# The end of a four-sublayer transformer kernel: last shared tile, late sums, row numbers and store queues rearranged

## The chip, the cores and the metric

The kernel runs on one core of one Trainium2 chip, in one launch. The metric is the device time of the whole program in microseconds (us). The engines of the core are TensorE (PE in the profile), VectorE (DVE), ScalarE (ACT), GpSimd (POOL) and SyncE (SP); each runs its own instruction stream, and they meet only at semaphores.

## What is computed

Two layers on 896 tokens of width 512, each a cross attention and a feed-forward part with residual sums. Only the last part, the mixture of experts of layer 1, matters here:

```
scores = softmax(t @ gate_w.T); weights, indices = top_k(scores, 2)
y = 0
for e in range(16):
    w_e = sum(where(indices == e, weights, 0))
    y = y + swiglu(t, w1[e], w3[e], w2[e]) * w_e
z = swiglu(t, sw1, sw3, sw2)
x = x + tanh(g_ffn[1]) * (y + z)
```

Every token goes to two of 16 experts (y) and through the shared pair of experts (z). All arithmetic is float32.

## The kernel before, in words

The 896 tokens are NT = 7 tiles of P = 128 rows; x, the residual and later the output, stays on chip as [128, 7, 512]. Before the experts run, each token row is scattered by expert into an array in DRAM (sorted_rows), so that the experts work on dense tiles of 128 rows, at least one for each expert; in this input there are 21.

One expert tile n goes through these hands. GpSimd loads its rows (`load`), ScalarE copies them (`place`), TensorE turns them (`rows_T`), multiplies (`up_expert`), turns the hidden rows (`hidden_T`) and multiplies again (`down_expert`). VectorE copies the result from PSUM to the one buffer yr (`tile_out`, semaphore d_sv). GpSimd then copies the tile's row numbers to to_row and issues an indirect DMA that scatters yr to y_dram, called token_rows in the profile (`scatter`, semaphore y_st). There is one yr and one to_row, so `tile_out(n)` waits until scatter n-1 has landed. The row numbers themselves were written by VectorE earlier (`row_ends`, semaphore row_read).

The shared experts' second product is `shared_part(t, ...)` on TensorE for token tile t: 18 matmuls of 512 columns (6 chunks of the inner width, three products each), which leave a sum in PSUM bank SHARED_BANK[t]. VectorE adds it to x in `shared_out(t)` (semaphore y_sv). Tiles 0 to 3 (BEFORE = 4) are multiplied around the start of the expert tiles, tiles 4 to 6 at TensorE's very end, after and between the last expert products. SHARED_BANK is (4, 5, 0, 1, 0, 1, 2), so tile 6 is alone in bank 2; still, `shared_part` waits at every t from 2 on for the shared_out two tiles back, for tile 6 that of tile 4.

Each token has two scattered results, j = 0 and j = 1. SyncE loads them back tile by tile: seven loads of 256 KB for j = 0 when all tiles but the last expert's have landed, seven for j = 1 when everything has (`back[t][j]`, semaphores back_ld). VectorE adds the seven of j = 0, then goes through the tiles for j = 1: for t below 4 only the add (semaphore out_st), for t = 4, 5 and 6 first `shared_out(t)` and then the add. SyncE stores each tile to out when out_st reaches it, and then waits for all seven stores.

The order on every engine is written out by hand in the code.

Of the kernel before, what the change touches and what calls it, by code (L numbers as in the profile page):

```python
# [28 lines left out]
P = 128  # L29
# [4 lines left out]
TOK = B * S  # L34
NT = TOK // P
# [17 lines left out]
BEFORE = 4  # L53
# [7 lines left out]
def flamingo(nc, x_in, ctx_in, mask_in, cols_in, rows_in, scal_in, wq0_in, wk0_in, wv0_in, wo0_in,  # L61
             gu0_in, wd0_in, wq1_in, wg1_in, wkv1_in, wo1_in, gate_in, sh13_in, sh2_in,
             e13_in, e2_in, out):
    with ExitStack() as stack:
# [3 lines left out]
        def sem(name):  # L68
            return stack.enter_context(nc.semaphore(name))
# [43 lines left out]
        x = nc.alloc_sbuf_tensor_at("x", [P, NT, D], F32, offset=x_base)  # L113
# [10 lines left out]
        def at(off, *dims, rows_=P):  # L124
            n = 1
            for d in dims:
                n *= d
            return shaped(arena[0:rows_, off:off + n], dims)
# [118 lines left out]
        back = [[at(28144 + t * D, D), at(4352 + t * D if t < 5 else 44288 + (t - 5) * D, D)] for t in range(NT)]  # L247
# [29 lines left out]
        y_dram = nc.dram_tensor("token_rows", (P + 2 * TOK, D), F32, kind="Internal").ap()  # L277
# [21 lines left out]
        x_ld = sem("x_ld")  # L299
# [89 lines left out]
        d_sv = sem("d_sv")  # L389
        y_st = sem("y_st")  # L390
# [3 lines left out]
        row_read = sem("row_read")  # L394
        to_set = sem("to_set")
        to_held = sem("to_held")
        back_add = sem("back_add")
        out_st = sem("out_st")
# [7 lines left out]
        back_ld = [[sem(f"back_ld{t}_{j}") for j in range(2)] for t in range(NT)]  # L406
# [3 lines left out]
        def counts(engine):  # L410

            return [engine.value_load(tile_count[0:1, i:i + 1], min_val=NE - 3 + i, max_val=ROWS_MAX - 3 + i)
                    for i in range(4)]
# [31 lines left out]
            return lnt0[:, n % 6, :] if n < NT else lnt1[:, n % NT % 4, :] if n < 2 * NT else lnt[:, n % 2, :]  # L445


        @block.sync
        def _(sp):

# [88 lines left out]
            tiles = sp.value_load(tile_count[0:1, 3:4], min_val=NE, max_val=ROWS_MAX)  # L539
            for j, landed in enumerate((last, tiles)):  # L540
                sp.wait_ge(y_st, landed * 16)
                for t in range(NT):
                    first = P + j * TOK + t * P
                    sp.dma_start(back[t][j], y_dram[first:first + P, :]).then_inc(back_ld[t][j], 16)
            out_t = out.rearrange("(t p) d -> t p d", p=P)
            for t in range(NT):
                sp.wait_ge(out_st, 1 + t)
                sp.dma_start(out_t[t], x[:, t, :]).then_inc(x_ld, 16)
            sp.wait_ge(x_ld, 16 * (NT + 1))
# [3 lines left out]
        def _(pe):  # L553
# [133 lines left out]
            for i in range(8):  # L687
                n, m = i // 4, i % 4
# [258 lines left out]
            pe.wait_ge(w_low, nth("sh2"))  # L947

            def shared_part(t, first, end):
                if first == 0 and t >= 2:  # L950
                    pe.wait_ge(y_sv, 3 * NT + t - 1)
                into = ps[:, SHARED_BANK[t], :]
                for m in range(first, end):
                    z = SH_CHUNKS[m]
                    if t == 0:
                        pe.wait_ge(hsh_low, m + 1)
                    h, w = ([half[0:z, t * P:(t + 1) * P] for half in hsh[m][:2]],
                            [half[0:z, m, :] for half in sh2[:2]])
                    if t >= BEFORE:
                        w[0] = sh2_kept[0:z, m, :]  # L960
                        if m == 4:
                            h[1] = h4_kept[0:z, (t - BEFORE) * P:(t - BEFORE + 1) * P]
                    mm(into, h[0], w[0], start=m == 0, stop=False)  # L963
                    mm(into, h[0], w[1], start=False, stop=False)
                    last = mm(into, h[1], w[0], start=False, stop=m == 5)
                if end == 6:
                    last.then_inc(y_mm, 1)

            for t in range(BEFORE - 1):
                shared_part(t, 0, 6)  # L970

            pe.wait_ge(tables_set, 1)
            last3, last2, last1, tiles = counts(pe)
# [36 lines left out]

            rows_T(0)
            shared_part(BEFORE - 1, 0, 3)
            up_expert(0)
            rows_T(1)
            shared_part(BEFORE - 1, 3, 6)
            hidden_T(0)
            with pe.Fori(1, last1) as n:
# [16 lines left out]
        def _(act):  # L1034
# [95 lines left out]
            for i in range(8):  # L1130
                n, m = i // 4, i % 4
# [128 lines left out]
            for i in range(8):  # L1260
                n, m = i // 4, i % 4
# [47 lines left out]
            last3, last2, last1, tiles = counts(act)  # L1309

            def rows_save(n):
                act.wait_ge(xg_tr, n + 1)
                fn(xgT, ps[:, 6, :].rearrange("p (k t) -> p k t", k=KC), ACT.Copy).then_inc(xg_sv, 1)

            def silu_tile(n):
                act.wait_ge(gu_mm, n + 1)
                fn(smoe, ps[:, 4, 0:EI], ACT.Silu).then_inc(m_silu, 1)
# [16 lines left out]
            silu_tile(last2)  # L1334
            rows_save(last1)
            silu_tile(last1)


        @block.vector
        def _(dve):  # L1340
# [448 lines left out]
            def shared_out(t):  # L1789
                dve.wait_ge(y_mm, 3 * NT + t + 1)  # L1790
                if t >= BEFORE:
                    dve.wait_ge(back_add, t + 1)
                v.scalar_tensor_tensor(x[:, t, :], ps[:, SHARED_BANK[t], :], tg[:, 3:4], x[:, t, :], ALU.mult, ALU.add
                                       ).then_inc(y_sv, 1)
# [5 lines left out]
            last3, last2, last1, tiles = counts(dve)  # L1800
# [49 lines left out]
            for t in range(NT):  # L1850
                dve.wait_ge(back_ld[t][0], 16)
                v.tensor_tensor(x[:, t, :], x[:, t, :], back[t][0], ALU.add).then_inc(back_add, 1)
            for t in range(NT):
                if t >= BEFORE:
                    shared_out(t)
                dve.wait_ge(back_ld[t][1], 16)
                if t < BEFORE:
                    dve.wait_ge(back_add, t + 1)
                else:
                    dve.wait_ge(y_sv, 3 * NT + t + 1)  # L1860
                v.tensor_tensor(x[:, t, :], x[:, t, :], back[t][1], ALU.add).then_inc(out_st, 1)
# [3 lines left out]
        def _(pool):  # L1865
# [24 lines left out]
            for i in range(8):  # L1890
                n, m = i // 4, i % 4
# [31 lines left out]
            last3, last2, last1, tiles = counts(pool)  # L1923
# [11 lines left out]
                load(n)  # L1935

            def scatter(n, stored=None):
                pool.wait_ge(d_sv, n + 1)
                if stored is not None:
                    pool.wait_ge(y_st, stored)  # L1940
                nc.gpsimd.tensor_copy(to_row[:], arena[:, bass.ds(A_TO + n % 4, 1)]).then_inc(to_set, 1)
                pool.wait_ge(to_set, n + 1)
                pool.sem_inc(to_held, 1)
                pool.indirect_dma_start(y_dram, bass.IndirectOffsetOnAxis(to_row[:, 0:1], 0), yr, None
                                        ).then_inc(y_st, 16)
# [4 lines left out]
            next_load(2)  # L1950
            next_load(3)
            scatter(0)
            next_load(4)
            scatter(1, 16)
            with pool.Fori(5, tiles) as n:
                next_load(n)
                scatter(n - 3, n * 16 - 48)
# [61 lines left out]
```

## Time and profile before

| | us |
|---|---|
| median of 3 runs | 962.27 |
| lowest and highest | 962.15, 965.42 |
| the profiled execution, its own time | 964.5 |
| its span, first to last instruction | 962.8 |
| TensorE busy in the span | 932.7 |

The profiled execution's own time lies 1.7 us above its span. The profile is of one execution, so durations from it are compared with that execution's time first and then set against the median.

### The profile page before, as it was taken

The numbers are of one execution on the slowest core, as the hardware profiler recorded it, in microseconds if no ns is written. First come the engines' busy times: TensorE is split into PE (matmuls) and PEld (weight loads), VectorE is DVE, ScalarE is ACT, GpSimd is POOL, SyncE is SP. The second block draws the span as 40 slices with busy tenths as digits, with TensorE's granted clock in tenths as the row PEclk, the third lists the DMA queues.
The fourth block names the chain that finished last, engine by engine and source line by source line (L and its number), as shares of the span: only waits on it lengthen the run. The fifth ranks groups of instructions, "written<-read, shape, count | busy, mean of one in ns | idle before, by whom it ended". The sixth has DMA issues, their size and how long they took to land.

```text
span 962.8 us, 17950 instructions
## 1 busy us (share of the span) xinstructions
PE 932.7 (97%) x7523; PEld 720.6 (75%) x7524; DVE 451.6 (47%) x755; ACT 303.0 (31%) x477; POOL 76.9 (8%) x110
## 2 busy tenths in 40 slices
PE   5999999999999999989999999999999999999995
PEld 5878787878788888779999544888798766666554
DVE  6665545455455456873221154597665122222224
ACT  4633333332332334653211121335532222222210
POOL 0000000000000003000000000112006112122210
PEclk9999999999999999999999999999999999999998
DMA  8000010101011012044000300840503449787534
GB/s 338 10 27 34 1 34 1 34 1 34 5 74 34 1 35 78 2 154 175 1 1 1 131 1 0 318 182 1 181 1 131 156 170 329 285 290 241 210 123 166
DMA packets 26773, 96.04 MB, mean 100 GB/s; under 512 B 3282, under 2 KB 4306, under 8 KB 23634
## 3 DMA queue, kind: packets, MB, share of 16 engines
q1 hardware_dynamic: 20354, 72.69, 21.3%
q0 software_dynamic: 6352, 22.35, 6.2%
q8 instruction: 55, 0.90, 0.4%
q14 instruction: 12, 0.10, 0.0%
HBM read 76.37 MB, written 18.66 MB: 99 GB/s over the span
## 4 chain that ended last, share of the span: by engine, by line
PE 88%; DVE 6%; ACT 3%; DMA 2%; issue 1%; SPq 0%; POOL 0%; POOLq 0%; DVEq 0%; ACTq 0%
PE ps L563 18%; PE ps L564 17%; PE ps L565 17%; PE ps L991 10%; PE ps L827 7%; PE ps L1001 5%; PE ps L643 4%; PE ps L626 4%; PE ps L849 1%; PE ps L982 1%; DMA land_c<-in_ctx 1%; PE ps L665 1%; PE ps L963 1%; PE ps L612 1%; PE ps L1008 1%
## 5 line engine op out<-in xcount | busy, mean ns | idle before, releaser
L563 PE MATMUL ps<-arena_r 128*125 128x512 f32 (+1 forms) x416 | 163.8, 394 | 4.2 <-DVE arena_r L1357 4.2
L564 PE MATMUL ps<-arena_r 128*125 128x512 f32 (+1 forms) x416 | 157.0, 377 | 0.0
L565 PE MATMUL ps<-arena_r 128*125 128x512 f32 (+1 forms) x416 | 156.8, 377 | 0.0
L563 PE MATMUL ps<-hT,arena_r 128*128 128x448 f32 (+1 forms) x368 | 136.3, 370 | 2.4 <-DVE arena_r L1376 1.1
L565 PE MATMUL ps<-hT,arena_r 128*128 128x448 f32 (+1 forms) x368 | 134.4, 365 | 0.0
L564 PE MATMUL ps<-hT,arena_r 128*128 128x448 f32 (+1 forms) x368 | 134.4, 365 | 0.0
L991 PE MATMUL ps<-arena 128*128 x336 | 102.9, 459 | 0.0
L1062 ACT ACTIVATE arena<-arena,mbias,mscale 125x448 f32<-125x448 f32 x96 | 66.2, 752 | 102.0 <-DVE arena L1484 101.9
L563 PEld LDWEIGHTS ps<-arena_r 128*125 128x125 f32 (+1 forms) x416 | 78.0, 188 | 21.8 <-DVE arena_r L1357 4.6
L565 PEld LDWEIGHTS ps<-arena_r 128*125 128x125 f32 (+1 forms) x416 | 77.9, 187 | 13.8
L564 PEld LDWEIGHTS ps<-arena_r 128*125 128x125 f32 (+1 forms) x416 | 78.1, 188 | 10.7
L991 PEld LDWEIGHTS ps<-arena 128*128 128x128 f32 x336 | 62.3, 190 | 31.2
L563 PEld LDWEIGHTS ps<-hT,arena_r 128*128 128x128 f32 (+1 forms) x368 | 68.3, 186 | 10.8 <-issue 1.9
L565 PEld LDWEIGHTS ps<-hT,arena_r 128*128 128x128 f32 (+1 forms) x368 | 68.3, 186 | 6.4
L564 PEld LDWEIGHTS ps<-hT,arena_r 128*128 128x128 f32 (+1 forms) x368 | 68.3, 186 | 6.1
L827 PE MATMUL ps<-arena 128*128 128x512 f32 x154 | 66.9, 592 | 0.0
L1484 DVE TENSOR_SCALAR arena<-ps 125x1344 f32<-125x1344 f32 x32 | 49.8, 1557 | 20.3 <-PE ps L626 20.0
L1001 PE MATMUL ps<-arena 128*128 (+1 forms) x126 | 57.7, 594 | 0.5 <-DVE arena L1819 0.5
L827 PEld LDWEIGHTS ps<-arena 128*128 128x128 f32 x154 | 28.9, 190 | 34.5 <-issue 34.4
L1616 DVE SCALAR_TENSOR_TENSOR arena<-ps,cols,arena 128x896 f32<-128x896 f32 x11 | 12.7, 1151 | 77.1 <-ACT arena L1218 77.1
L1808 DVE SCALAR_TENSOR_TENSOR arena<-ps,arena 128x352 f32<-128x352 f32 x21 | 12.3, 584 | 73.2 <-PE ps L991 47.0
L643 PEld LDWEIGHTS ps<-arena 125*32 125x32 f32 x1536 | 35.7, 110 | 12.0 <-issue 11.6
(224 smaller groups left out, 1167.0 us busy)
## 6 DMA issues: line engine op xcount, KB each, us to landing
arena<-in_e SPq DMA_DIRECT2D x16, 1408.0 KB, 6.6
arena<-in_e SPq DMA_DIRECT2D x16, 512.0 KB, 7.4
sorted_rows<-arena POOLq DMA_DIRECT2D x1, 7453.0 KB, 34.0
land_c<-in_ctx SPq DMA_DIRECT2D x8, 752.0 KB, 4.2
arena<-sorted_rows POOLq DMA_DIRECT2D x21, 257.0 KB, 6.1
land_w<-in_gu SPq DMA_DIRECT2D x8, 512.0 KB, 5.3
arena<-token_rows SPq DMA_DIRECT2D x14, 256.0 KB, 4.5
arena<-in_e SPq DMA_DIRECT2D x16, 192.0 KB, 8.8
```

Of the source, the lines that this page charges most:

```text
L563: mm(into, a[0], w[0], start=i == 0, stop=False)
L564: mm(into, a[0], w[1], start=False, stop=False)
L565: last = mm(into, a[1], w[0], start=False, stop=i == len(operands) - 1)
L626: last = mm(ps[0:TP, h, c * S:(c + 1) * S], kT[key_half][r, g, c * TP:(c + 1) * TP], queries[query_half][r, b, g, :], start=i == 0, stop=i ...
L643: last = mm(ps[h * HD:(h + 1) * HD, 7, first:first + S], w, probs[g % 2][:, h, c * S:(c + 1) * S], start=c == 0, stop=c == TC - 1)
L827: last = mm(into, h0[m][:, t * P:(t + 1) * P], wd0[:, m, :], start=m == 0, stop=m == MC - 1)
L991: last = mm(ps[:, 4 + j, 0:EI], xgT[:, k, :], arena[:, bass.ds(w + (k * 2 * EI + j * EI), EI)], start=k == 0, stop=k == KC - 1)
L1001: last = mm(ps[:, 3, :], hmoeT[0:z, c, :], arena[0:z, bass.ds(w + (2816 + c * D), D)], start=c == 0, stop=c == 2)
L1062: done = fn(p, p, ACT.Exp, bias=mbias[:, b * 3 + c:b * 3 + c + 1], scale=mscale[:, b * 3 + c:b * 3 + c + 1])
L1484: v.tensor_scalar(probs[g % 2], ps[0:TP, 0:HG, 0:TC * S], -CLIP / SCALE, CLIP / SCALE, ALU.max, ALU.min).then_inc(clipped, 1)
L1616: v.scalar_tensor_tensor(into[0:size].rearrange("p (n t) -> p n t", n=2), ps[0:size, 4 * (1 - m % 2) + 2:4 * (1 - m % 2) + 4, 0:HALF], sca ...
L1808: v.scalar_tensor_tensor(hmoe[:, 0:EI], ps[:, 5, 0:EI], weight, smoe, ALU.mult, ALU.mult).then_inc(m_h, 1)
```

## The change

Four edits, all in the program's last 30 us or so and in the code that the expert tiles share:

1. `shared_part(6)` no longer waits for `shared_out(4)`.
2. VectorE does `shared_out(4)` and `shared_out(5)` right after the seven adds of j = 0, ahead of all adds of j = 1. `shared_out(6)` stays where it was.
3. GpSimd's `scatter(n)` waits first for row_read (the row numbers are written) and for the scatter before, makes to_row, and only then waits for d_sv (the result is in yr). One more increment of to_held, for which nobody waits, stands between; the DMA follows the second one.
4. The loads of j = 1 and the stores of the odd tiles (1, 3, 5) are issued by ScalarE, those of the even tiles (0, 2, 4, 6) by SyncE.

```diff
--- before.py
+++ after.py
@@ -539,11 +542,10 @@
             for j, landed in enumerate((last, tiles)):
                 sp.wait_ge(y_st, landed * 16)
-                for t in range(NT):
+                for t in range(0, NT, 1 + j):
                     first = P + j * TOK + t * P
                     sp.dma_start(back[t][j], y_dram[first:first + P, :]).then_inc(back_ld[t][j], 16)
-            out_t = out.rearrange("(t p) d -> t p d", p=P)
-            for t in range(NT):
+            for t in range(0, NT, 2):
                 sp.wait_ge(out_st, 1 + t)
                 sp.dma_start(out_t[t], x[:, t, :]).then_inc(x_ld, 16)
             sp.wait_ge(x_ld, 16 * (NT + 1))
@@ -947,7 +949,7 @@
             def shared_part(t, first, end):
-                if first == 0 and t >= 2:
+                if first == 0 and 2 <= t < NT - 1:
                     pe.wait_ge(y_sv, 3 * NT + t - 1)
@@ -1335,6 +1337,14 @@
             rows_save(last1)
             silu_tile(last1)
 
+            act.wait_ge(y_st, tiles * 16)
+            for t in range(1, NT, 2):
+                first = P + TOK + t * P
+                act.dma_start(back[t][1], y_dram[first:first + P, :]).then_inc(back_ld[t][1], 16)
+            for t in range(1, NT, 2):
+                act.wait_ge(out_st, 1 + t)
+                act.dma_start(out_t[t], x[:, t, :]).then_inc(x_ld, 16)
+
@@ -1850,8 +1860,10 @@
             for t in range(NT):
                 dve.wait_ge(back_ld[t][0], 16)
                 v.tensor_tensor(x[:, t, :], x[:, t, :], back[t][0], ALU.add).then_inc(back_add, 1)
+            for t in range(BEFORE, NT - 1):
+                shared_out(t)
             for t in range(NT):
-                if t >= BEFORE:
+                if t == NT - 1:
                     shared_out(t)
                 dve.wait_ge(back_ld[t][1], 16)
@@ -1935,11 +1947,13 @@
             def scatter(n, stored=None):
-                pool.wait_ge(d_sv, n + 1)
+                pool.wait_ge(row_read, n + 1)
                 if stored is not None:
                     pool.wait_ge(y_st, stored)
                 nc.gpsimd.tensor_copy(to_row[:], arena[:, bass.ds(A_TO + n % 4, 1)]).then_inc(to_set, 1)
                 pool.wait_ge(to_set, n + 1)
+                pool.sem_inc(to_held, 1)
+                pool.wait_ge(d_sv, n + 1)
                 pool.sem_inc(to_held, 1)
                 pool.indirect_dma_start(y_dram, bass.IndirectOffsetOnAxis(to_row[:, 0:1], 0), yr, None
                                         ).then_inc(y_st, 16)
```

On VectorE, at the end of the program, the last rows of its stream before read so (L1861 is the add of j = 1, L1793 is `shared_out`):

```order
L1861 TENSOR_TENSOR x<-x,arena 128x512 [waits back_add,back_ld0_1]
L1861 TENSOR_TENSOR x<-x,arena 128x512 [waits back_add,back_ld1_1]
L1861 TENSOR_TENSOR x<-x,arena 128x512 [waits back_add,back_ld2_1]
L1861 TENSOR_TENSOR x<-x,arena 128x512 [waits back_add,back_ld3_1]
L1793 SCALAR_TENSOR_TENSOR x<-ps,tg,x 128x512 [waits back_add,y_mm]
L1861 TENSOR_TENSOR x<-x,arena 128x512 [waits y_sv,back_ld4_1]
L1793 SCALAR_TENSOR_TENSOR x<-ps,tg,x 128x512 [waits back_add,y_mm]
L1861 TENSOR_TENSOR x<-x,arena 128x512 [waits y_sv,back_ld5_1]
L1793 SCALAR_TENSOR_TENSOR x<-ps,tg,x 128x512 [waits back_add,y_mm]
L1861 TENSOR_TENSOR x<-x,arena 128x512 [waits y_sv,back_ld6_1]
```

and in the changed kernel so (L1873 is the add, L1803 `shared_out`):

```order
L1803 SCALAR_TENSOR_TENSOR x<-ps,tg,x 128x512 [waits back_add,y_mm] x2
L1873 TENSOR_TENSOR x<-x,arena 128x512 [waits back_add,back_ld0_1]
L1873 TENSOR_TENSOR x<-x,arena 128x512 [waits back_add,back_ld1_1]
L1873 TENSOR_TENSOR x<-x,arena 128x512 [waits back_add,back_ld2_1]
L1873 TENSOR_TENSOR x<-x,arena 128x512 [waits back_add,back_ld3_1]
L1873 TENSOR_TENSOR x<-x,arena 128x512 [waits y_sv,back_ld4_1]
L1873 TENSOR_TENSOR x<-x,arena 128x512 [waits y_sv,back_ld5_1]
L1803 SCALAR_TENSOR_TENSOR x<-ps,tg,x 128x512 [waits back_add,y_mm]
L1873 TENSOR_TENSOR x<-x,arena 128x512 [waits y_sv,back_ld6_1]
```

Two of the three `shared_out` now stand ahead of the first add of j = 1; the third still stands between the last two adds.

On GpSimd, one turn of the expert loop's scatter and the scatter after the loop read before (L1941 makes to_row, L1944 is the indirect DMA):

```order
L1940 REGISTER_ALU [waits d_sv]
L1941 ISA [waits y_st]
L1941 COPY to_row<-arena 128x1
L1944 DMA token_rows<-arena,to_row 1920x512 [waits to_set]
L1955 REGISTER_ALU
L1955 COMPARE_AND_BRANCH
L1938 REGISTER_ALU
```

and now:

```order
L1952 REGISTER_ALU [waits row_read]
L1953 ISA [waits y_st]
L1953 COPY to_row<-arena 128x1
L1958 DMA token_rows<-arena,to_row 1920x512 [waits to_set,d_sv]
L1969 REGISTER_ALU
L1969 COMPARE_AND_BRANCH
L1950 REGISTER_ALU
```

The wait for the result has moved from ahead of the copy of the row numbers to behind it, directly ahead of the DMA.

## Rows read from the trace of the kernel before

**Rows 1.** The page: its span, and busy time by engine.

```profile
span 962.8 us, 17950 instructions
PE 932.7 (97%) x7523; PEld 720.6 (75%) x7524; DVE 451.6 (47%) x755; ACT 303.0 (31%) x477; POOL 76.9 (8%) x110
```

**Rows 2.** The chain that ended last, its end: start us, us, what.

```profile
934.56 0.70 DVE arena L1825
...
936.54 3.54 DMA token_rows<-arena,to_row
...
940.10 0.70 DVE arena L1825
...
942.25 2.98 DMA token_rows<-arena,to_row
...
946.57 4.88 DMA arena<-token_rows
...
952.08 0.76 DVE x L1793
...
959.73 0.69 DVE x L1861
```

**Rows 3.** Timeline of TensorE, 945.5 to 958.5: start us, us, what [idle before].

```profile
945.95 0.39 PE L965 MATMUL ps<-arena_r 96*128 96x512 f32 x1
952.88 0.80 PE L963 MATMUL ps<-arena_r 128*128 128x512 f32 x1 [6.54 <-DVE x L1793]
...
958.44 0.39 PE L965 MATMUL ps<-arena_r 96*128 96x512 f32 x1
```

**Rows 4.** Timeline of VectorE, 940 to 955, same columns.

```profile
940.71 4.29 DVE L1852 TENSOR_TENSOR x<-x,arena 128x512 f32<-128x512 f32 x7
947.82 1.38 DVE L1861 TENSOR_TENSOR x<-x,arena 128x512 f32<-128x512 f32 x2 [2.81 <-DMA arena<-token_rows]
...
954.39 0.69 DVE L1861 TENSOR_TENSOR x<-x,arena 128x512 f32<-128x512 f32 x1
```

**Rows 5.** Timeline of GpSimd, 935 to 943, same columns.

```profile
936.54 0.98 POOL L1944 DMA_INDIRECT token_rows<-arena,to_row  x1 [0.82 <-POOL to_row L1941]
941.07 0.36 POOL L1941 CAST to_row<-arena 128x1 uint32 x1 [3.55 <-DVE arena L1825]
942.25 1.20 POOL L1944 DMA_INDIRECT token_rows<-arena,to_row  x1 [0.82 <-POOL to_row L1941]
```

**Rows 6.** The line of the j = 1 loads, in two windows: issues 4 and 5, issues 6 and 7.

```profile
L544 SPq DMA_DIRECT2D arena<-token_rows x2: 432/432/432, 946.6 to 947.0; - x2
DMA to landing us min/median/max: 4.9/5.1/5.3
...
L544 SPq DMA_DIRECT2D arena<-token_rows x2: 432/432/433, 947.5 to 948.0; - x2
DMA to landing us min/median/max: 5.5/5.6/5.7
```

**Rows 7.** The line of the stores, in two windows: the sixth, then the seventh and last.

```profile
L548 SPq DMA_DIRECT2D out_x<-x x1: 333/333/333, 955.1 to 955.1; - x1
DMA to landing us min/median/max: 2.4/2.4/2.4
...
L548 SPq DMA_DIRECT2D out_x<-x x1: 332/332/332, 960.4 to 960.4; - x1
DMA to landing us min/median/max: 2.0/2.0/2.0
```

**Rows 8.** Stretches of 1 us; the last three columns: granted TensorE clock, DMA share, GB/s.

```profile
949.00:950.00 1.00, 0.00 (x0) 0.00 (x0) 0.19 (x1) 0.00 (x0) 0.00 (x0) 0.70 0.84 191
...
952.00:953.00 1.00, 0.12 (x1) 0.12 (x1) 0.90 (x3) 0.00 (x0) 0.00 (x0) 0.50 1.07 410
...
956.00:957.00 1.00, 1.00 (x5) 0.83 (x4) 0.00 (x0) 0.00 (x0) 0.00 (x0) 0.89 0.76 291
```

More of the change, by code:

```diff
@@ L445, in ln_tile @@
             return lnt0[:, n % 6, :] if n < NT else lnt1[:, n % NT % 4, :] if n < 2 * NT else lnt[:, n % 2, :]
+        out_t = out.rearrange("(t p) d -> t p d", p=P)
         @block.sync
```

## The prediction

> **What bounds the kernel now.** I read the page first: TensorE is busy 97% of a span of 962.8 us [rows 1], so for most of the program only TensorE's work counts, and none of it is removed here. The change can pay only where TensorE stops being the bound. The chain that ended last says where that is: up to 934 us it is nothing but products, and from 934.56 on it leaves TensorE [rows 2]. I read that tail as four links, each with a term below.
>
> First, two scatters in a row. VectorE copies a result to yr at 934.56 (0.70 us), GpSimd's indirect DMA starts at 936.54 and lands 3.54 us later, at 940.08; only then may VectorE copy the last result (940.10 to 940.80), whose DMA starts at 942.25 and lands 2.98 us later, at 945.23 [rows 2]. Second, the loads of j = 1. SyncE issues them from 945.25 on; the fourth, issued at 946.57, lands 4.88 us later, at 951.45 [rows 2]. Third, the chain passes through TensorE once more: `shared_out(4)` at 952.08 (0.76 us) releases the product of shared tile 6, which starts at 952.88 after TensorE had stood idle for 6.54 us, and its last matmul starts at 958.44 and lasts 0.39 us [rows 2, 3]. Fourth, `shared_out(6)`, the last add from 959.73 to 960.42, and the last store, issued at 960.45, 2.0 us to landing [rows 2, 7]. That is 962.45, and the span ends at 962.8.
>
> **Part 1 and 2: tile 6's product, and shared_out(4) and (5) early.** TensorE ends tile 5's product at 945.95 + 0.39 = 946.34 [rows 3]. Without the wait, 18 matmuls follow at once. Before they took 952.88 to 958.83, 5.95 us, in part at a granted clock of 0.50, the lower of TensorE's two levels (1.2 of 2.4 GHz), into which it had fallen during the idle time (0.70 in the us from 949, 0.50 from 952) [rows 3, 8]. So tile 6 is done by 952.3 at worst, and earlier where the clock does not fall. I need only that it is done before VectorE asks for it.
>
> VectorE's own line is then rebuilt from its rows. The j = 0 adds end at 940.71 + 4.29 = 945.0 [rows 4]. `shared_out(4)` fits from 945.0 to 945.8. `shared_out(5)` needs tile 5's product (946.34), so it runs from about 946.4 to 947.2. The first load of j = 1 had its add at 947.82, after 2.81 us of idle time [rows 4]: both edits lie inside that gap and cost nothing. If the first load landed earlier than 947.2, `shared_out(5)` would show, by the difference.
>
> From there the landings rule. Load 4 (t = 3) lands at 951.45; load 5 at 947.04 + 5.3 = 952.3; load 6 at 947.5 + 5.5 = 953.0; load 7 at 948.0 + 5.7 = 953.7 [rows 2, 6]. An add is 0.69 us (two took 1.38) [rows 4]. So add 4 runs 952.3 to 953.0, add 5 953.0 to 953.7, `shared_out(6)` to 954.45, add 6, with the gap of 0.1 us that stands between `shared_out(6)` and the last add now (959.63 to 959.73), to 955.2. Before it ended at 960.42. **This term is 5.2 us at the add.**
>
> **The last store.** It took 2.0 us where nothing else moved, the sixth 2.4 us behind others [rows 7]. The engines of the DMA queues are full from 952 (share 1.07, 410 GB/s) and still carry 291 GB/s in the us from 956 [rows 8]. Seven loads and six stores of 0.262 MB are 3.41 MB, and the last of it lands at 955.11 + 2.4 = 957.5. A seventh store that comes 1.5 us behind the sixth's place adds at 410 GB/s 0.64 us, of which the slack in the us from 956 (119 GB/s under full, 0.12 MB, 0.29 us) takes a part. I take a landing at 957.7, against 962.45: 4.75 us, where the add alone said 5.2. Bounds: 5.2 (nothing in the way, landing at 957.25), and 3.35 if the last two stores, 0.52 MB, go at the 191 GB/s of the us from 949 [rows 8] instead of 410: 2.7 us instead of 1.3, landing at 959.1.
>
> **Part 3: row numbers ahead of the result.** The handoff from the end of VectorE's copy to the DMA's start is 936.54 - 935.26 = 1.28 us for the second last scatter and 942.25 - 940.80 = 1.45 us for the last [rows 2]. In it stand the wait, the copy of the row numbers (0.36 us in the last) and 0.82 us from that copy to the DMA [rows 5]. The 0.82 stays, since the DMA is still issued behind a semaphore and an increment: now it follows VectorE's copy directly. That leaves 1.28 - 0.85 = 0.43 and 1.45 - 0.85 = 0.60, together 1.0 us. In the last scatter the row copy may start only at 940.08 less 0.43, when the scatter before has landed, beside VectorE's copy of 0.70 us; it starts about 0.3 us after its release (as 941.07 after 940.80) and takes at most 0.36, so it is done at +0.66, just ahead of the result at +0.72. The second increment is the unknown: below, the row copy's own 0.82 us might have to pass before the wait for d_sv is even looked at, and then the last scatter starts at +0.66 + 0.82 or later, and gains nothing or loses up to 0.7; above, 1.28 + 1.45 - 2 x 0.6 = 1.5 if the 0.82 shrinks too. I take 1.0, because in the second last scatter at least GpSimd stands idle long before and the row copy is hidden whole. Everything behind the last scatter, the j = 1 loads first, moves up by it.
>
> The same rule is written down. The Trainium skill, "SBUF — State Buffer", in "SBUF: two separate sides", says that a VectorE operation with two SBUF inputs and a GpSimd operation that reads SBUF exclude each other for a whole instruction. The trace agrees with it as far as one row goes: the row copy that lay beside VectorE's adds took 0.36 us [rows 5]. By that rule the copy would now lie beside a copy out of PSUM and be shorter, which helps to hide it; by the row it is 0.36 and hidden too, by 0.06 us.
>
> In the other 19 expert tiles the scatter leaves 0.4 us earlier as well. TensorE does not wait for it there, so this is worth 0. `next_load` stands behind the scatter on GpSimd's queue and its rows are needed a tile later, so nobody is hurt by the wait for row_read, which was fulfilled a tile before.
>
> **Part 4: two queues.** SyncE needs 0.43 us an issue [rows 6]; seven issues took 945.25 to 948.4. The seventh load landed 5.7 us after its issue, so the issue was not what it waited for, and the engines that carry the packets are shared. I take 0. The trace has no DMA from ScalarE, so the bounds are those of a gain and a loss: if the slow us from 949 (191 GB/s) ran at 410 [rows 8], the loads would land earlier, but then VectorE's own line sets the end: it is free at 947.2, and seven adds, one `shared_out` and a gap (4.85 + 0.75 + 0.1) end at 952.9, where the landings, moved up by 1.0, gave 954.2. So the gain is 0 to 1.3 us. ScalarE has been idle since its last silu; its three issues cost nobody anything. Loss: the pairs of loads share the engines, so t = 0 lands when t = 1 did; hidden behind `shared_out(5)` up to 0.6 us of it.
>
> **The sum.** 4.75 + 1.0 + 0 = 5.75 us. Profiled execution: 964.5 - 5.75 = 958.75, its span 957.1. The median lies 2.2 us under the profiled execution, so 962.27 - 5.75 = **956.5 us**, 0.6% less. A measurement of this kernel can tell about 0.5%, 4.8 us, from no change; the forecast is just past it.
>
> **Rivals.**
> A, the forecast: the landings of the j = 1 loads and then the last store set the end; 5 to 6.6 us gained, 955.7 to 957.3. Chance 0.58.
>
> B, the DMA backlog takes the gain: all 14 transfers now come without the pause that TensorE's product made. If the slow stretch (191 GB/s in the us from 949 [rows 8]) comes again while the stores run, or the last store shares with three others, it lands 1 to 2.5 us later than I take it; with a row handoff that gives nothing, another 1 us. 3 to 4.8 us gained, 957.5 to 959.3. For it: the queue was at share 1.07 just there. Against: the sixth store took only 2.4 us. Chance 0.22.
>
> C, the second queue fills the slow stretch: VectorE becomes the bound, 6.6 to 7.6 us gained (5.75 + 1.3 and what the store finds free), 954.7 to 955.7. For it: share 0.84 at 191 GB/s means that engines were waiting on something, not moving [rows 8]. Against: other packets from the same engines would wait on the same thing. Chance 0.14. The Trainium skill, "DMA: Bandwidth & Descriptors", "Issuing engines are not separate DMA queues", says that starting DMAs from several engines saves only the time of issuing. By that rule C does not happen, and the sum stays at 956.5; no row here shows a second issuing queue.
>
> D, the same or slower: ScalarE's queue, used here for the first time, starts late. VectorE takes the tiles in order, so a late t = 1 holds everything. Behind its landing stand six adds, one shared_out, a gap and the store: 4.1 + 0.75 + 0.1 + 2.0 = 7 us. It is slower than before when t = 1 lands later than 962.45 - 7 = 955.5, which is 8 us after the landing of 947.4 that the shift gives; a landing 13 us late would be 967 us. No DMA of this tail took longer than 5.7 us. Within 0.5% either way 0.03, slower 0.03.
>
> **How the numbers follow.** Faster by over 0.5% means under 957.46: A and C whole, and a little of B's edge: 0.73. Same: most of B and half of D: 0.24. Slower 0.03. The range leaves out D and the far halves of B and C: 954.6 to 958.8, 4.2 us.
>
> **What would show it.** TensorE's 6.54 us of idle time gone and tile 6's product ended before 952.3; the DMA of the last scatter 0.8 to 0.9 us after VectorE's copy ends, and landing near 944.2; `shared_out(4)` and (5) ahead of 947.3; VectorE waiting for the loads of t = 2 to 5 still, and the last add ending near 954.2; the last store taking 2.0 to 2.7 us. Wrong it would be if ScalarE's loads land after those of SyncE that were issued later, if the last store takes over 3.5 us, or if the DMA follows its row copy later than 0.85 us.

## The result, and the profile after

| | before | changed |
|---|---|---|
| median, us (9 runs each) | 965.42 | 959.25 |
| lowest and highest | 962.15, 965.93 | 955.27, 961.04 |
| the profiled execution | 964.5 | 955.72 |
| its span | 962.8 | 954.1 |

The ratio is 0.9936, with a 95% interval of 0.9914 to 0.9959: 0.64% faster, 6.2 us of 965.42. The forecast gain was 5.75 us (ratio 0.994), but it was taken from the median of the three runs then shown, 962.27, and the kernel before has moved to 965.42 with six more runs. So the forecast time, 956.5 us with a range up to 958.8, missed the measured 959.25. The ratios and medians here leave out three runs far above the others of their kernel (976.9, 1043.7 and 2390.5 us).

The two profiles differ by more than the kernels do, 8.7 us. I cut them where TensorE ceases to be the bound: VectorE's copy of the second last expert result starts at 934.56 before [rows 2] and at 932.61 after. Of the 8.7 us, 1.95 lie ahead of that cut, where the change touches nothing on the path; the tail behind it shrank from 28.3 to 21.5 us, by 6.8.

The page after:

```profile
span 954.1 us, 17972 instructions
PE 929.8 (97%) x7523; PEld 718.5 (75%) x7524; DVE 451.1 (47%) x755; ACT 303.1 (32%) x477; POOL 76.6 (8%) x110
...
q1 hardware_dynamic: 19490, 71.11, 21.0%
q0 software_dynamic: 6352, 22.35, 6.3%
q10 hardware_dynamic: 864, 1.57, 0.4%
```

Compare [rows 1]: TensorE's own work is 2.9 us less with the same instructions, so part of the difference is its clock (the experiments come back to this). A new queue, q10, carries ScalarE's six transfers, 1.57 MB.

VectorE's tail after, in its timeline (answers to [rows 4]):

```profile
932.61 0.69 DVE L1835 COPY arena<-ps 128x512 f32<-128x512 f32 x1 [1.54 <-PE ps L1003]
...
937.44 0.69 DVE L1835 COPY arena<-ps 128x512 f32<-128x512 f32 x1 [3.67 <-DMA token_rows<-arena,to_row]
938.04 4.29 DVE L1862 TENSOR_TENSOR x<-x,arena 128x512 f32<-128x512 f32 x7
942.26 0.74 DVE L1803 SCALAR_TENSOR_TENSOR x<-ps,tg,x 128x512 f32<-128x512 f32 x1
944.44 0.75 DVE L1803 SCALAR_TENSOR_TENSOR x<-ps,tg,x 128x512 f32<-128x512 f32 x1 [1.44 <-PE ps L967]
945.37 2.52 DVE L1873 TENSOR_TENSOR x<-x,arena 128x512 f32<-128x512 f32 x4 [0.18 <-DMA arena<-token_rows]
948.48 1.29 DVE L1873 TENSOR_TENSOR x<-x,arena 128x512 f32<-128x512 f32 x2 [0.60 <-DMA arena<-token_rows]
949.69 0.74 DVE L1803 SCALAR_TENSOR_TENSOR x<-ps,tg,x 128x512 f32<-128x512 f32 x1
950.53 0.69 DVE L1873 TENSOR_TENSOR x<-x,arena 128x512 f32<-128x512 f32 x1
```

`shared_out(4)` and (5) (L1803) now lie in the gap ahead of the first load, and the last `shared_out` no longer waits for TensorE. Four adds run in one piece: the loads that they need are all there. Before, VectorE had to wait for the third and the fourth.

GpSimd's timeline (answers to [rows 5]) and TensorE's last matmul (to [rows 3]):

```profile
934.12 0.98 POOL L1958 DMA_INDIRECT token_rows<-arena,to_row  x1 [4.48 <-DVE arena L1835]
937.60 0.19 POOL L1953 CAST to_row<-arena 128x1 uint32 x1 [2.50 <-DMA token_rows<-arena,to_row]
938.95 1.24 POOL L1958 DMA_INDIRECT token_rows<-arena,to_row  x1 [1.16 <-DVE arena L1835]
```

```profile
948.14 0.39 PE L967 MATMUL ps<-arena_r 96*128 96x512 f32 x1
```

The DMA is now released by VectorE's copy: 933.30 to 934.12 and 938.13 to 938.95, 0.82 us each, where it was 1.28 and 1.45. TensorE is done at 948.53, before VectorE asks for tile 6 at 949.69.

The seventh load (SyncE's fourth), then the last store, by line and window (answers to [rows 6, 7]):

```profile
L547 SPq DMA_DIRECT2D arena<-token_rows x1: 432/432/432, 943.3 to 943.3; - x1
DMA to landing us min/median/max: 5.8/5.8/5.8
...
L550 SPq DMA_DIRECT2D out_x<-x x1: 332/332/332, 951.3 to 951.3; - x1
DMA to landing us min/median/max: 2.4/2.4/2.4
```

The seventh load lands 7.1 us after the first was issued (941.99), against 8.4 before. And the stretches of 1 us while the loads and first stores are under way (the last column is GB/s; answers to [rows 8]):

```profile
944.00:945.00 1.00, 1.00 (x6) 0.82 (x5) 0.56 (x1) 0.00 (x0) 0.00 (x0) 1.00 0.99 361
945.00:946.00 1.00, 1.00 (x6) 0.83 (x5) 0.82 (x3) 0.00 (x0) 0.00 (x0) 1.00 1.05 399
946.00:947.00 1.00, 1.00 (x7) 0.81 (x6) 1.00 (x3) 0.00 (x0) 0.00 (x0) 1.00 0.99 346
947.00:948.00 1.00, 1.00 (x6) 0.83 (x5) 0.88 (x2) 0.00 (x0) 0.00 (x0) 1.00 1.06 406
```

The slow stretch of before (191 GB/s in the us from 949) is gone.

### The profile page after: what moved, and what is told of

It reads as the page before. It is cut to its first block, busy times and chain, and to the rows that moved or that the text cites. A ratio compares the mean times of both kernels' runs of the same rounds, so it can differ in the third digit from the quotient of the medians.

```text
span 954.1 us, 17972 instructions
## 1 busy us (share of the span) xinstructions
PE 929.8 (97%) x7523; PEld 718.5 (75%) x7524; DVE 451.1 (47%) x755; ACT 303.1 (32%) x477; POOL 76.6 (8%) x110
## 3 DMA queue, kind: packets, MB, share of 16 engines
q0 software_dynamic: 6352, 22.35, 6.3%
q10 hardware_dynamic: 864, 1.57, 0.4%
## 4 chain that ended last, share of the span: by engine, by line
PE 88%; DVE 6%; ACT 3%; DMA 2%; issue 1%; SPq 0%; DVEq 0%; POOLq 0%; ACTq 0%
PE ps L565 18%; PE ps L566 17%; PE ps L567 17%; PE ps L993 10%; PE ps L829 7%; PE ps L1003 5%; PE ps L645 4%; PE ps L628 4%; PE ps L851 1%; PE ps L984 1%; PE ps L667 1%; PE ps L614 1%; DMA land_c<-in_ctx 1%; PE ps L1010 1%; DMA token_rows<-arena,to_row 1%
```

## The experiments

Besides the tail I use a second measure, from the first j = 1 load's issue to the end of the span ("last stretch"). It leaves out the scatters, whose landing took from 3.3 to 4.1 us with no edit between. Before it is 945.25 to 962.84, 17.6 us; after 941.99 to 954.08, 12.1 us.

**again.** The changed kernel once more.

> The changed kernel once more. The tail is measured in every profile as the time from VectorE's copy of the second last expert result to the end of the span: 28.24 us before (934.56 to 962.8), 21.49 us after (932.61 to 954.1). Theory 1 (the tail was forecast about rightly, and the level of both kernels' runs, 962 to 966 and 955 to 961 us, is set upstream by falls of TensorE's clock that differ from run to run): tail within 0.5 us of 21.5, ratio 0.992 to 0.995, and the runs of one kernel split by 3 to 5 us, the long ones with the lower mean clock (0.995 to 0.997) and the short ones with 0.999 or 1.000. Theory 2 (the change itself made the slow runs of 959 to 961 us, by DMA contention at the end): slow runs at an unchanged mean clock, and a profile with a tail over 24 us.

Median 958.62 us (7 runs, 956.2 to 961.29), before, run beside it, 964.49 (15 runs, 962.22 to 967.72), ratio 0.9938 (0.9914 to 0.9962). Tail 22.35 us, 0.9 over the first profile and so outside the 0.5 us that theory 1 allowed it: the second last scatter took 4.07 us to land, against 3.29. The last stretch, which leaves the scatters out, is 12.2 us against 12.1. The ratio repeats. The runs of one kernel again spread over 5 us; their mean clock is 0.995 to 0.997, and that a short run has a clear clock did not hold here (956.2 us had 0.996). The nine runs of the result showed the other half: 955.27, 955.72 and 955.99 us had 0.999 or 1.000. So theory 2 has nothing for it here (no tail over 24 us). Of theory 1, the last stretch repeats, the tail only within the scatters' landing, and the cause of the spread is not yet shown.

**one_queue.** The changed kernel without edit 4.

```diff
-                for t in range(0, NT, 1 + j):
+                for t in range(NT):
...
-            for t in range(0, NT, 2):
+            for t in range(NT):
                 sp.wait_ge(out_st, 1 + t)
...
-            act.wait_ge(y_st, tiles * 16)
...
```

> The changed kernel with all loads of j = 1 and all stores on SyncE again. Theory 1 (the second queue takes away the slow stretch of the loads): the seventh load lands 8.4 us after the release as before instead of 7.1, a stretch under 250 GB/s comes back, tail 22.3 to 22.8 us, 0.8 to 1.3 us more than 21.5. Rival (the slow stretch is a matter of the run, queues are worth nothing): tail 21.2 to 21.8 us.

Last stretch 942.74 to 956.48, 13.7 us, against 12.0 to 12.4 in all six profiles of the new order with both loads and stores on two queues. Its windows:

```profile
944.00:945.00 1.00, 1.00 (x6) 0.83 (x5) 0.00 (x0) 0.00 (x0) 0.00 (x0) 1.00 0.91 320
945.00:946.00 1.00, 1.00 (x6) 0.83 (x5) 0.89 (x2) 0.00 (x0) 0.00 (x0) 1.00 0.94 346
946.00:947.00 1.00, 1.00 (x6) 0.80 (x6) 1.00 (x2) 0.00 (x0) 0.00 (x0) 1.00 1.01 227
947.00:948.00 1.00, 1.00 (x6) 0.84 (x5) 0.72 (x2) 0.00 (x0) 0.00 (x0) 1.00 0.84 297
948.00:949.00 1.00, 1.00 (x6) 0.64 (x4) 0.67 (x2) 0.00 (x0) 0.00 (x0) 1.00 0.93 287
```

The slow stretch is back: 227 to 297 GB/s for 3 us. Theory 1 holds in the profile, though the tail of 23.2 us is over the 22.3 to 22.8 that I gave it. In the timed runs it does not show: median 958.12, ratio 0.9938 (0.9916 to 0.996), the same as for again. 1.6 us are 0.17%, less than that interval.

**keep_wait.** The changed kernel with tile 6's wait back, `if first == 0 and t >= 2:`.

> The changed kernel with tile 6's wait for shared_out(4) back. Since shared_out(4) now stands ahead of the last adds and is done before TensorE ends tile 5's product, theory 1 says that the wait is already fulfilled: no idle time of TensorE, tail 21.3 to 21.7 us, so that edit 1 is worth nothing beside edit 2. Rival (the wait still bites, as shared_out(4) comes behind the j = 0 adds that wait for their loads): TensorE idle for 1 us or more ahead of tile 6, tail longer only if VectorE then waits for its sum.

Tail 21.75 us, last stretch 12.1, no idle time of TensorE ahead of tile 6; median 956.0 (6 runs), ratio 0.9917 (0.989 to 0.9944). Edit 1 is worth nothing beside edit 2, as theory 1 says. That this median lies 2.6 us under that of again goes with the clock and not with the wait: four of these six runs had a mean clock of 0.999, and none of again's seven.

**late_rows.** The changed kernel with the old order in `scatter`.

> The changed kernel with the row numbers made behind the wait for the result, as before. Theory 1: both handoffs from VectorE's copy to the DMA go back from 0.82 to 1.28 and 1.45 us, all behind them 1.1 us later, tail 22.4 to 22.8 us. Rival (shared_out(5) and TensorE's end hide part of it, as VectorE waits for tile 5's product until 944.4 while loads land from 945.4): only 0.9 us or less is seen, tail 22.0 to 22.3.

GpSimd's timeline:

```profile
937.13 0.18 POOL L1953 CAST to_row<-arena 128x1 uint32 x1 [5.60 <-DVE arena L1835]
938.13 0.98 POOL L1956 DMA_INDIRECT token_rows<-arena,to_row  x1 [0.82 <-POOL to_row L1953]
942.41 0.36 POOL L1953 CAST to_row<-arena 128x1 uint32 x1 [3.30 <-DVE arena L1835]
943.59 1.20 POOL L1956 DMA_INDIRECT token_rows<-arena,to_row  x1 [0.82 <-POOL to_row L1953]
```

With VectorE's copies ending at 936.84 and 942.13 the handoffs are 1.29 and 1.46 us again, 1.1 us more than 2 x 0.82. Tail 22.43 us, ratio 0.9942 (0.992 to 0.9964). The tails of two profiles of the changed kernel differ by 0.9 us, so the tail alone would prove nothing; the handoffs do.

**wait_alone** and **sums_alone.** The kernel before with edit 1 alone, and with edit 2 alone.

```diff
-                if first == 0 and t >= 2:
+                if first == 0 and 2 <= t < NT - 1:
```

```diff
+            for t in range(BEFORE, NT - 1):
+                shared_out(t)
             for t in range(NT):
-                if t >= BEFORE:
+                if t == NT - 1:
                     shared_out(t)
```

> The kernel before with edit 1 alone (tile 6 without its wait). Tail 28.28 us before. My reckoning: tile 6's product follows tile 5's at once, shared_out(4), (5) and (6) stay between the last adds, so VectorE ends with add 4, shared_out(5), add 5, shared_out(6), add 6 in a row, at 3.6 to 3.9 us less than before: tail 24.3 to 24.8. Rival (the landings of the loads hide the three sums too): tail 23.0 to 23.5.

> The kernel before with edit 2 alone (shared_out(4) and (5) ahead of the last adds), and tile 6 still with its wait. Since the wait is fulfilled as soon as shared_out(4) is done, theory 1 says that this alone gives all that the two edits give: no idle time of TensorE, tail 23.0 to 23.6 us (28.28 less 4.75 to 5.2). Rival (the two are needed together): TensorE idle by several us, tail 25 or more.

The end of VectorE's timeline in wait_alone:

```profile
951.99 0.75 DVE L1793 SCALAR_TENSOR_TENSOR x<-ps,tg,x 128x512 f32<-128x512 f32 x1
952.84 0.69 DVE L1861 TENSOR_TENSOR x<-x,arena 128x512 f32<-128x512 f32 x1
953.45 0.75 DVE L1793 SCALAR_TENSOR_TENSOR x<-ps,tg,x 128x512 f32<-128x512 f32 x1
954.30 0.69 DVE L1861 TENSOR_TENSOR x<-x,arena 128x512 f32<-128x512 f32 x1
```

and in sums_alone:

```profile
950.55 1.39 DVE L1863 TENSOR_TENSOR x<-x,arena 128x512 f32<-128x512 f32 x2 [0.30 <-DMA arena<-token_rows]
951.86 0.74 DVE L1793 SCALAR_TENSOR_TENSOR x<-ps,tg,x 128x512 f32<-128x512 f32 x1
952.70 0.69 DVE L1863 TENSOR_TENSOR x<-x,arena 128x512 f32<-128x512 f32 x1
```

From the first load's issue (943.47 and 943.35) to the end of the last add it is 11.5 us in wait_alone and 10.0 in sums_alone, against 15.2 before: 3.7 and 5.1 us gained. Edit 2 alone gives 5.1 of the forecast's 5.2 us, and TensorE has no idle time there. The last store gives back a part: it took 3.0 us to land in sums_alone, so that its last stretch is 13.5 us, 4.1 us under before. By the tail, wait_alone (24.4 us) is where I put it; sums_alone (24.35) is outside my 23.0 to 23.6, by a scatter that landed in 3.73 us (3.54 before) and by that store. Each of these two kernels, and of the three that follow, has one timed run, its profiled one (959.04 and 958.48 us here, then 958.41, 957.21 and 961.6), so only the profiles speak for them.

**split_loads, split_stores** and **queues_alone.** Which half of edit 4 helps, and what it gives by itself: only the loads on two queues, only the stores, and the kernel before with edit 4 alone.

> The changed kernel with the odd loads of j = 1 on ScalarE, but all seven stores on SyncE. From the release (the first load's issue) to the end of the span it takes 12.1 us with both split (12.09, 12.16 and 12.14 in three profiles) and 13.8 with one queue. Theory Q1 (the slow stretch comes while the loads alone are under way, and a second queue of loads fills it): no us under 350 GB/s between the first data and the last load, last add ended 9.2 to 9.4 us after the release, stretch 12.0 to 12.5 us. Rival Q2 (what helps is that stores do not queue behind loads): slow stretch back, 13.3 to 13.8 us.

> The changed kernel with all loads of j = 1 on SyncE and the odd stores on ScalarE. Theory Q1: us under 300 GB/s behind the first two loads, last add ended 9.9 to 10.3 us after the release, stretch 13.2 to 13.8 us. Rival Q2: 12.0 to 12.5 us.

> The kernel before with edit 4 alone. The loads land faster, but the end hangs on the chain shared_out(4), tile 6's product, shared_out(6), last add, last store. shared_out(4) stands behind the fourth add, which now comes up to 1 us earlier (9.2 against 10 us at the end of the adds, part of it before the fourth). So 16.6 to 17.3 us from the release to the end, against 17.6 before. Rival (the second queue is worth its 1.7 us here too): 15.9 us.

| j = 1 loads / stores | last stretch, us | to the end of the last add | GB/s, third to fifth us of data |
|---|---|---|---|
| one / one (one_queue) | 13.7 | 10.3 | 227, 297, 287 |
| one / two (split_stores) | 13.9 | 10.5 | 231, 285, 211 |
| two / one (split_loads) | 13.1 | 10.2 | 379, 348, 385 |
| two / two (again) | 12.2 | 9.3 | 389, 356, 397 |

The us of data are counted from the first with over 100 GB/s. The slow stretch goes with the loads: it stands in all six profiles with one queue of loads, and in none of the eight with two. That part of Q1 is right. But split_loads gains only 0.6 of the 1.6 us: its fifth to seventh loads landed up to 6.9 us after their issue, and VectorE waited 1.63 us for them, while the first stores went out. So neither theory is right alone: on one profile of each split, the 1.6 us come only when both loads and stores are split. Why a single queue of loads dips below 300 GB/s in its third us the runs do not show. queues_alone has 16.8 us, inside what was expected: 0.8 us gained, so that the chain through TensorE hides half of edit 4.

**filled** and **filled_before.** What makes the runs of one kernel differ by 5 us. TensorE waits 3.1 us for a layer norm at about 419 us in every profile, and behind that wait its clock is at 0.50 in some profiles and at 1.00 in others. The stretches (the third last column is the granted clock) in the profile of before:

```profile
424.00:425.00 1.00, 1.00 (x6) 0.90 (x5) 0.96 (x5) 0.25 (x1) 0.00 (x0) 0.50 0.40 49
425.00:426.00 1.00, 1.00 (x4) 0.81 (x3) 0.96 (x2) 0.35 (x1) 0.00 (x0) 0.50 0.77 270
426.00:427.00 1.00, 1.00 (x3) 0.78 (x3) 0.96 (x4) 0.41 (x1) 0.00 (x0) 0.50 0.99 397
```

and after:

```profile
424.00:425.00 1.00, 1.00 (x6) 0.79 (x6) 0.96 (x2) 0.00 (x0) 0.00 (x0) 1.00 0.83 254
425.00:426.00 1.00, 1.00 (x6) 0.82 (x5) 0.96 (x4) 0.42 (x1) 0.00 (x0) 1.00 0.97 373
```

3.4 us at half the clock cost about 1.7 us (an estimate, half of the stretch), and before had it where the changed kernel's profile had none. Its wait also ended 1.0 us later, at 422.1 against 421.1. Together that is more than the 1.95 us by which the two profiles differ ahead of the tail, so a part was made up behind. In late_rows the stretch was 6.8 us. The edit fills the wait with a product that nobody reads:

```diff
             to_tokens(5, output_of_0)
+            output_of_0(5, ps[:, ln_bank(NT + 3), :])
             ln_transposes(NT + 3)
```

> The changed kernel, and on TensorE twelve matmuls more (the product of token tile 5 once again, into the bank that the next transposes overwrite; its result is never read) in the 3.13 us for which TensorE waits for a layer norm at about 419 us. Theory U (the spread of the runs upstream comes from a fall of the clock to 0.50 for 3.4 or 6.8 us right behind that wait, at 423 us, in 4 of 6 profiles so far; half of it is lost, 1.7 or 3.4 us): no fall near 423 us in the profile, runs at 953.5 to 956.5 us with mean clock 0.998 or 0.999, ratio to before near 0.991. Rival V (the clock falls by chance, or because of heat or the load of the chip): falls still there, in the products behind, runs spread over 955 to 961 as before, ratio 0.993 to 0.994.

> The kernel before with the same twelve filler matmuls. Theory U: no fall near 423 us, median 1.5 to 3 us under that of before (ratio 0.997 to 0.9985), runs at 960.5 to 963 us. The tail keeps its 28.2 us with the 6.5 us of idle time ahead of tile 6. Rival V: ratio 1.000, runs up to 967.

filled: median 955.63 us (7 runs, up to 957.17, where I had said 956.5), before, run beside it, 964.46 (17 runs), ratio 0.9897 (0.9861 to 0.9933; the two medians alone would give 0.9908). filled_before: median 962.7 (12 runs), ratio 0.9981 (0.9969 to 0.9994), as theory U said, but its runs reach 964.58, where I had said 963. Its tail is 29.4 us and not 28.2: the second last scatter took 4.09 us, and tile 6's product 6.8 us, most of it at half the clock. In filled TensorE's wait has shrunk, and the clock stays up:

```profile
420.01 0.40 PE L567 MATMUL ps<-arena_r,hT 128*128 128x512 f32 x1
420.75 0.66 PE L667 MATMUL ps<-ident,arena 128*128 128x128 f32 x4 [0.34 <-DVE arena L1406]
```

```profile
423.00:424.00 1.00, 1.00 (x6) 0.79 (x5) 0.96 (x3) 0.59 (x1) 0.00 (x0) 1.00 0.66 102
424.00:425.00 1.00, 1.00 (x6) 0.83 (x5) 0.96 (x3) 0.00 (x0) 0.00 (x0) 1.00 0.98 385
```

**filled_again**, the same kernel on another chip.

> The kernel filled once more, on whatever chip this call gets. Theory U: runs of 954 to 957.5 us, ratio to before 0.989 to 0.992, no fall of the clock near 423 us in the profile. Rival V (the first time was luck): fall there, runs up to 961, ratio 0.993 to 0.994.

Median 955.97 us (6 runs, 955.45 to 957.94), ratio 0.9917 (0.99 to 0.9934), no fall. In all, 7 of 11 profiles without the filler show the fall behind the wait, and none of 3 with it. The 13 runs of filled lie in 954.7 to 957.9 with clocks of 0.998 to 1.000; the 16 runs of the changed kernel in 955.3 to 961.3, 13 of them with 0.995 to 0.997. Their medians are 955.9 and 958.7 us. Theory U holds. The two were not run side by side; before, which was run beside each, had medians of 965.4 and 964.5 beside the changed kernel and of 964.5 and 964.9 beside filled.

The traces show what may be a second piece of the spread; no edit tests it. TensorE's first matmuls follow each other at half the later pace, and the moment at which the pace doubles differs between executions. Two neighbouring matmuls of the same shape and of the same product, 15 us after the start, in late_rows and then in queues_alone:

```profile
15.12 0.52 PE L566 MATMUL ps<-arena_r 128*128 128x376 f32 x1
15.44 0.52 PE L567 MATMUL ps<-arena_r 128*128 128x376 f32 x1
```

```profile
15.05 0.34 PE L564 MATMUL ps<-arena_r 128*128 128x376 f32 x1
15.23 0.34 PE L565 MATMUL ps<-arena_r 128*128 128x376 f32 x1
```

The pace doubles at 19.0 us in late_rows and at 15.0 in queues_alone, and TensorE's wait for that layer norm ends at 422.4 and at 420.2. Over the eleven profiles without the filler the two times go together (correlation 0.94), so that the start would account for up to 2.2 us.

## Why the prediction was right in its steps and wrong in its time

**The step that failed** is the last line of the sum: "The median lies 2.2 us under the profiled execution, so 962.27 - 5.75 = 956.5". It takes the median of three runs as the kernel's level. One of those three was 965.42, and the profile showed the granted clock at half for 3.4 us at 423 us, which I did not look for, since it lies 510 us ahead of the change. With six more runs the same kernel's median is 965.42, and 965.42 x 0.994 would have been 959.7, against 959.25 measured. The range was built from rivals about the tail alone and had no term for the spread of the runs. filled and filled_before show that the fall behind that wait is a large part of it (1.8 us of before's median, 2.8 of the changed kernel's). What spreads the rest of before's runs (961.1 to 964.6 even when filled) stays open in part: the scatters' landing is one piece, up to 0.8 us in the profiles, and the start of the program may be another, up to 2.2 us. The measured 959.25 also lies outside rival A's 955.7 to 957.3 and inside rival B's 957.5 to 959.3, but by the level alone: the measured gain of 6.2 us is A's (5 to 6.6), not B's (3 to 4.8).

**Tile 6's product and the early sums.** Right: 5.2 us at the last add, and sums_alone measures 5.1. I joined the two edits in one term; the runs show that edit 2 alone carries it, since `shared_out(4)` is done before TensorE comes to tile 6, and that the removed wait gives 3.7 us without it and nothing with it. Two signs that I named came out otherwise. VectorE no longer waits for the loads of t = 2 to 5, only for the first and the fifth (0.18 and 0.60 us). And the last scatter's DMA follows its row copy by 1.16 us, over my 0.85, which says nothing against the step: it waited for the result, and starts 0.82 us behind it.

**The last store.** Its size was off with one queue: 3.0 us to landing in sums_alone and in one_queue, so that the last stretch gained 4.1 and 3.9 us there instead of 4.75. With two queues it took 2.4.

**Row numbers.** Right, 1.0 forecast, 0.46 + 0.63 = 1.09 measured; the second increment costs nothing that shows. The copy of the row numbers took 0.19 us in the last scatter, beside a copy out of PSUM, and 0.36 beside adds with two SBUF inputs, in late_rows as well. The rule of the Trainium skill, "SBUF — State Buffer", "SBUF: two separate sides", agrees with these lengths.

**Two queues.** I took 0; it is 1.6 us once the chain through TensorE is gone (13.7 against 12.1). That is rival C's slow stretch, filled: 1.0 to 1.1 us of it come at the last add (10.3 us against 9.2 and 9.3), inside the 0 to 1.3 that I allowed there, and the rest at the stores. But VectorE did not become the bound, as C said; it still waits 0.4 to 0.9 us for the fifth load in the six profiles. The Trainium skill, "DMA: Bandwidth & Descriptors", "Issuing engines are not separate DMA queues", says that issuing from several engines saves only issue time. The seventh load's landing alone would agree with it: issued 1.4 us sooner, it lands 1.3 us sooner. The rates do not: in one_queue the us from 946 to 949 carry 227 to 297 GB/s, though the last load is issued at 945.5, against 356 to 397 in again. The measurement decides.

**The tail's sum.** 1.09 (handoffs), 0.2 (landings of the two scatters), 5.9 (first load's issue to the last add: 15.2 to 9.2) and -0.4 (last add to the end: 2.4 to 2.9) are 6.8 us. I had 5.75, 1.0 too little: too little by the queues' 1.6 and by 0.3 in the handoffs and landings, too much by 0.9 in the adds and the last store (3.9 us gained in one_queue where I had 4.75). Rival B, a backlog that takes the gain, did not come. Nor did D: ScalarE's first load landed 3.8 us after its issue.

## What to carry to other kernels

Look at the granted clock of the whole span, and at every short wait of TensorE, before taking a level from a few runs: here a wait of 3 us far from the change was worth 1.8 to 2.8 us where the change was worth 6, and a filler product in it removed the fall in three profiles of three. When a wait is removed, ask whether another edit already fulfils it; one of the two may be free to stay. And where many loads of rows of 2 KB meet at the end of a program, try two issuing queues for loads and stores both, on the trace rather than on a rule. Here that gave 1.6 us in the profiles, too little for the timed runs to show.

## What the runs showed that was not expected

One queue of seven 256 KB loads from DRAM falls to 191 to 297 GB/s in its third to fifth us of data, in six profiles of six; with a second queue the same us carry 346 to 410 GB/s, in eight of eight. Why, no run shows. And the same wait of 3.1 us let TensorE's clock fall behind it in 7 profiles and left it at 1.00 in 4, with the same instructions around it. The Trainium skill, "TensorE: Matmul & The Clock Gate", "Part 1", says that the slow matmuls at the start of one kernel vary in number from run to run. The profiles agree for the start (the pace doubles at 15 to 19 us), and show the same in the middle of a program, with falls of 0, 3.4 and 6.8 us at this one place.
